# Compressed attention in 49 steps of 128 queries over both images, the local value bias in the output bias, value rows and late casts on ScalarE

## What is computed

```python
blk = mean of feat over 8 x 8 blocks                      # 49 per image
_, idx = lax.top_k(scores, 4); K_sel = blk[idx]
y_cmp = _mha(Q, blk, blk, wq_w[0], ..., pj_w[0], pj_b[0])  # 8 heads of 16 channels, softmax over 49
y_sel = _mha(Q, K_sel, K_sel, wq_w[1], ..., pj_b[1])       # softmax over 4
q = _lin(Q, wq_w[2], wq_b[2]); k = _lin(patches, wk_w[2], wk_b[2]); v = _lin(patches, wv_w[2], wv_b[2])
y_win = _lin(softmax(q k * scale) v, pj_w[2], pj_b[2])     # each pixel to its 7 x 7 neighbours
g = softmax(_lin(_ln(Q), g_w, g_b))
y = g[..., 0:1] * y_cmp + g[..., 1:2] * y_sel + g[..., 2:3] * y_win + Q
```

## Time and profile before

| | us |
|---|---|
| median of three runs (lowest to highest) | 770.14 (766.46 to 771.43) |
| the profiled execution: device time, span of its instructions | 772.19, 770.4 |
| busy in the span: TensorE, VectorE, ScalarE, GpSimd | 689.2, 607.4, 351.2, 214.8 |
| gates and projections end, first maximum of the compressed attention | 121.1 |
| last add of the compressed attention ends | 330.9 |

### The profile page before, as it was taken

The page is one execution under the profiler, slowest core; times in us unless marked ns, Lnnn a source line. Parts: engine busy times, 40 slices in busy tenths (PEclk is TensorE's granted clock), DMA queues, the critical chain, the costliest instruction groups (busy, mean ns, idle before and its releaser), DMA issues.

```text
span 770.4 us, 14139 instructions
## 1 busy us (share of the span) xinstructions
PE 689.2 (89%) x5055; PEld 365.3 (47%) x5055; DVE 607.4 (79%) x1236; ACT 351.2 (46%) x618; POOL 214.8 (28%) x331
## 2 busy tenths in 40 slices
PE   4998987789788989878999999999889999999996
PEld 2543443445344444444555555555434545455553
DVE  6996657878788799867777777777369879999873
ACT  2175423444444344305555555555534062646676
POOL 2026112545445454507100110010190436400000
PEclk9999988979999899969999999999999999999998
DMA  6004221533233339724656656762000000000101
GB/s 245 0 0 109 54 54 45 132 80 79 71 81 93 81 95 252 176 72 131 158 154 180 180 156 167 181 171 47 18 2 0 1 0 0 1 21 22 42 22 63
DMA packets 52663, 66.22 MB, mean 86 GB/s; under 512 B 10606, under 2 KB 48498, under 8 KB 50738
## 3 DMA queue, kind: packets, MB, share of 16 engines
q1 hardware_dynamic: 49426, 43.08, 21.3%
q10 hardware_dynamic: 3168, 22.24, 10.5%
HBM read 43.03 MB, written 21.57 MB: 84 GB/s over the span
## 4 chain that ended last, share of the span: by engine, by line
PE 50%; DVE 22%; issue 8%; ACT 6%; DMA 2%; POOL 1%; SPq 0%; ACTq 0%; DVEq 0%; POOLq 0%
PE banks L959 12%; PE banks L897 7%; PE banks L881 6%; PE banks L840 5%; DVE AC L1204 4%; DVE mx L1392 4%; PE banks L914 3%; DVE sm L1407 2%; DVE X L1484 2%; PE banks L852 2%; DVE SEB L1395 1%; PE banks L710 1%; ACT pf L1022 1%; ACT PTB L1067 1%; PE banks L782 1%
## 5 line engine op out<-in xcount | busy, mean ns | idle before, releaser
L1083 ACT ACTIVATE P<-banks 126x480 f32<-126x480 f32 (+2 forms) x196 | 101.1, 521 | 112.1 <-PE banks L881 98.6
L959 PE MATMUL banks<-FP,PTB 128*128 128x392 f32 x384 | 129.8, 493 | 2.1 <-DVE c L1487 1.2
L1456 DVE TENSOR_REDUCE wn<-banks 128x4 f32<-128x728 f32 x112 | 102.1, 913 | 26.0 <-PE banks L840 24.2
L1204 DVE SCALAR_TENSOR_TENSOR AC<-XT,vec,AC 128x1540 f32<-128x1540 f32 (+5 forms) x48 | 118.0, 2462 | 1.1
L959 PEld LDWEIGHTS banks<-FP,PTB 128*128 128x128 f32 x384 | 72.7, 190 | 56.9 <-DVE FP L1524 2.2
L549 POOL TENSOR_TENSOR SEB<-SEB,rg 112x392 f32<-112x392 f32 x112 | 61.2, 567 | 111.2 <-DVE rg L1414 111.2
L1058 ACT ACTIVATE SEB<-SEB 112x424 f32<-112x424 f32 x56 | 31.2, 558 | 113.1 <-DVE SEB L1395 113.1
L897 PE MATMUL banks<-P,Vw 126*17 126x120 f32 (+2 forms) x1568 | 73.3, 260 | 0.0
L519 POOL TENSOR_TENSOR pk<-pr,pk 128x434 bf16<-128x434 f32 (+1 forms) x42 | 47.7, 1136 | 45.4 <-DVE pk L1307 45.4
L804 PE MATMUL banks<-PTB,VP 106*128 106x448 f32 x112 | 54.0, 570 | 6.2 <-issue 3.7
L782 PE MATMUL banks<-Af,XT 128*112 128x424 f32 x112 | 54.2, 568 | 0.0
(11 more groups left out here) (247 smaller groups left out, 1195.6 us busy)
## 6 DMA issues: line engine op xcount, KB each, us to landing
k_parts<-pk SPq DMA_DIRECT2D x84, 108.5 KB, 3.4
Vw<-v_rows SPq DMA_DIRECT2D x84, 66.9 KB
q_parts<-pk SPq DMA_DIRECT2D x42, 112.0 KB, 2.3
K<-k_parts ACTq DMA_DIRECT2D x7, 651.0 KB, 5.8
v_rows<-vst SPq DMA_DIRECT2D x14, 263.5 KB
X<-in_x SPq DMA_DIRECT2D x2, 1568.0 KB, 8.3
K<-k_parts ACTq DMA_DIRECT2D x7, 434.0 KB, 3.7
out_y<-zs SPq DMA_DIRECT2D x7, 392.0 KB, 2.4
```

The lines of the kernel that those rows point to most:

```text
L959: last = mm(bank(2 + place_in_unit, C, ZPIX), WT[:, dy, part, C * grp:C * (grp + 1)], D[:, part, QROWS * q + dy:QROWS * (q + 1) + dy, :].r ...
L1083: a(P[q % 4][0:BKEYS[b], 0:4 * BQ[b]], PS[0:BKEYS[b], 4 + q % 2, 0:4 * BQ[b]], ACT.Exp).then_inc(sem("w_exp"), 1)
L1204: return ve.scalar_tensor_tensor(out=o, in0=src(ro + dy, rn, co + dx, cn), scalar=v(wcol + t), in1=o, op0=ALU.mult, op1=ALU.add)
L1456: ve.tensor_reduce(dst, src, AX.X, ALU.max, negate=True).then_inc(sem("w_slot_read"), 1)
```

## The change

- The compressed attention runs over both images as one row of 6272 pixels, in 49 tiles of 128 (`QT`), in groups of four tiles (512 columns, one bank); the last group has one tile, and one tile and one group have pixels of both images, and take their matmuls in two parts. `G`, the gates' transposes and logits follow: 13 groups instead of 14 bands.
- The local value bias is no longer added to each value row. As softmax weights sum to one, it is folded through the output projection into that projection's bias row, by two small matmuls and one add before the stage. `BV2` goes.
- Value rows are copied by ScalarE (no bias, one instruction per group), and ScalarE takes the second part's cast of late keys, two steps behind the projection; the third part on GpSimd stands three steps behind, as do the stores.
- Late jobs, keys and values in one list (`LATE_TURN`), stand in 37 steps and take banks 6 and 7 in turn. The residual stands behind the maxima and subtraction in VectorE's step. `pr` has four buffers.

The core of the diff:

```diff
+QT = 128
+CT = IMAGES * PIX // QT
+GROUP = 4
-        LATE_STEPS = 40
-        late_at = {NGJ + n: n * LATE_STEPS // NLATE for n in range(NLATE)}
-        vlate_at = {late_at[NGJ + j * 7 // 4]: j for j in range(NVJ)}
+        LATE_STEPS = 37
+        LATE_BANKS = (6, 7)
+        LATE_TURN = "kkvkkvkkvkv"
+        late = []
+        for n in range(NPJ - NGJ + NVJ):
+            kind = LATE_TURN[n % len(LATE_TURN)]
+            number = sum(which == kind for which, _, _ in late) + (NGJ if kind == "k" else 0)
+            late.append((kind, number, n * LATE_STEPS // (NPJ - NGJ + NVJ)))
...
@@ TensorE
-                    mm(bank(0, 124, C), ones[0:1, 0:124], row[0:1, 2 * C:3 * C], start=True, stop=True)
+                    for u in range(2):
+                        mm(bank(0, VH, C), v(V_FOLD + VH * u, VH), w("pj2", C, C * u), start=(u == 0), stop=(u == 1))
...
+                for n, kind, number in late_jobs(step):
+                    if n < 2:
+                        pe.wait_ge(sem("proj_read"), NGJ)
+                        pe.wait_ge(sem("g_stored"), NCG)
+                    elif late[n - 2][0] == "k":
+                        pe.wait_ge(sem("proj_read"), late[n - 2][1] + 1)
+                    else:
+                        pe.wait_ge(sem("v_ready"), late[n - 2][1] + 1)
+                    if kind == "k":
+                        project(number, LATE_BANKS[n % 2])
+                    else:
+                        values(number, LATE_BANKS[n % 2])
...
@@ ScalarE
+            def late_second(n):
+                cols = pjobs[n][3]
+                act.wait_ge(sem("residual"), n + 1)
+                a(pk[n % RING][:, SLOT[1], 0:cols], pr[n % RING][:, 0:cols], ACT.Copy).then_inc(sem("late_second"), 1)
+            def value_rows(j, b0):
+                vm, g, k = vjobs[j]
+                act.wait_ge(sem("vals"), j + 1)
+                if j >= 2:
+                    act.wait_ge(sem(f"v_stored{j % 2}"), 16 * (j // 2))
+                o = vst[j % 2][:, 0:k, :].rearrange("p t (j d) -> p (t j) d", d=VH)[:, :, 0:DH]
+                a(o, PS[0:124, b0, 0:C * k].rearrange("p (t d) -> p t d", d=DH), ACT.Copy).then_inc(sem("v_ready"), 1)
...
@@ VectorE
-            def value_rows(j):
...
-                for t in range(k):
-                    last = ve.tensor_tensor(o[:, HEADS * t:HEADS * (t + 1), :], i0[:, HEADS * t:HEADS * (t + 1), :],
-                                            BV2[:].rearrange("p (j d) -> p j d", j=HEADS), ALU.add)
-                last.then_inc(sem("v_ready"), 1)
...
-                    link(ve.tensor_copy(BV2[:], PS[0:124, 0, 0:C]))
+                    bias_row = W[0:VH, WCOL["pj2"]:WCOL["pj2"] + C]
+                    link(ve.tensor_tensor(bias_row, bias_row, PS[0:VH, 0, 0:C], ALU.add))
```

More of the change, by code:

```diff
@@ L819, in _, with scores @@
-            run_loop(pe, c_body, BANDS, True)
-            pe.wait_ge(sem("c_added"), NGRP)
+            def scores(s):
+                if s >= 2:
+                    pe.wait_ge(sem("c_sub"), s - 1)
+                for img, lo, hi in image_parts(QT * s, QT * (s + 1)):
+                    o = PS[lo - QT * s:hi - QT * s, s % 2, 0:SC]
+                    mm(o, XTB[:, lo:hi], Af[img][:], start=True, stop=False, skip_group_check=True)
+                    last = mm(o, on3[:, 0:hi - lo], E3[img][:], start=False, stop=True, skip_group_check=True)
+                last.then_inc(sem("c_s"), 1)
@@ new lines, in turned, with folded_values @@
+            def turned(s):
+                pe.wait_ge(sem("c_norm"), 2 * s + 2)
+                if s >= 2:
+                    pe.wait_ge(sem("c_pt"), s - 1)
+                for j in range(PAIRS):
+                    last = tr(bank(2 + s % 2, KC, QT, QT * j), Pn[s % 2][:, KC * j:KC * (j + 1)], ident)
+                last.then_inc(sem("c_tr"), 1)
+            def folded_values(g, j):
+                cols = group_cols(g)
+                if j == 0:
+                    if g == 1:
+                        pe.wait_ge(sem("g_rows"), 1)
+                    pe.wait_ge(sem("c_pt"), min(GROUP * (g + 1), CT))
+                    if g >= 2:
+                        pe.wait_ge(sem("c_added"), g - 1)
+                for part, (img, lo, hi) in enumerate(image_parts(cols.start, cols.stop)):
+                    last = mm(bank(4 + g % 2, C, hi - lo, lo - cols.start), VP[img][:, j, :], PT[g % 2][:, j, lo - cols.start:hi - cols.start],
+                              start=(j == 0 and part == 0), stop=(j == PAIRS - 1), skip_group_check=True)
+                if j == PAIRS - 1:
+                    last.then_inc(sem("c_vp"), 1)
@@ new lines, in _ @@
+            for step in range(C_STEPS):
+                if tile_at(step, 0) is not None:
+                    scores(step)
+                if tile_at(step, TURN_LAG) is not None:
+                    turned(step - TURN_LAG)
+                for g, j in vp_at.get(step, ()):
+                    folded_values(g, j)
+                for n, kind, number in late_jobs(step):
+                    if n < 2:
[7 more added lines that the diff above has]
+                        project(number, LATE_BANKS[n % 2])
+                    else:
+                        values(number, LATE_BANKS[n % 2])
+                if step == 1:
+                    pe.wait_ge(sem("gates"), 1)
+                    tr(bank(TURN_BANK, CT, QT), G[:, :, 2], ident).then_inc(sem("g_turned"), 1)
@@ L823, in _ @@
+            pe.wait_ge(sem("c_added"), NCG)
             pe.wait_ge(sem("masks"), 16 * 2 * BUFS)
```

431 lines of the change are left out of this document (192 added, 239 removed).

## The result

The changed kernel takes 729.75 us (median of 4 runs, 727.30 to 730.72) against 769.21 us (766.46 to 771.43): a ratio of 0.948, 95% interval 0.944 to 0.952. The profiled execution took 729.38 us, with a span of 727.6. The forecast was 728, and its range, 716 to 743, holds the result. But two of its sums are off by about 5 us each, in opposite directions: the stage ends 4.6 us earlier than foretold, and the part behind it is 5.7 us longer.

A forecast was written before the change was run, and what follows sets the result against it. VectorE and a loop of waits bound the steps with late jobs, VectorE the rest. 120.3 + 128 + 27.7 + 10 = 286 us for the stage's end, 45 less; 772.2 - 45 gives 727, plus 1 traffic: 728 us, range 716 to 743.

The forecast's parts named there:

- TensorE paces the first part: Steps with late key and value jobs mixed in: TensorE longest, 128 us for 37 steps; likeliest case, 0.69.
- Its sum, 119.3: TensorE's work in the 37 steps with late jobs, if it never waits: 119.3 us, 3.22 a step.
- The allowance of 9 us: Added to TensorE's 119.3 us: 3 for the low clock at the start, 6 for steps where VectorE is late.
- VectorE's sum, 102: VectorE's work in the 37 steps: 137.55 less 26.6 for casts and additions, less four steps of 2.35: 102 us.
- ScalarE's sum, 91: ScalarE's work in the 37 steps, with late casts and value copies added: 91 us, so TensorE stays longest.
- the 14.2 us of waiting for the high part: VectorE's wait for ScalarE before residuals, expected to vanish once residuals stand behind the next step's maximum and subtraction.
- the step's length from latencies: Rival: 4.02 us a step comes from loop latencies, so 37 steps cost 149; 749 us, cases between 738 and 752; 0.15.
- Start, second part and end: First maximum at 120.3; 11 steps after the late jobs, 27.7 us; last maximum to last add into XT, 10 us.
- The store ring: Four high-part buffers, reused after stores: slack 2 to 3 us, cost 0 to 5 us, within the likeliest range.
- What is late next: Window start: mask loads land at + 36.1 after tile 37's maximum, first window matmul at + 38.9; fits by 2.8 us.
- The window "as it is": Window stage and the rest: left unchanged, 1 us (0 to 4) added for load traffic; wrong if changed over 4 us.
- Slower by the low clock: Rival: shorter waits keep TensorE at its lower clock while late jobs run, 119.3 becoming 239; some 839 us; 0.02.

The follow-up runs named there:

- the two cuts: Changed kernel without the small second matmul of each tile's scores: 715.3 us; changed kernel with late residuals covering 16 of 434 columns: 727.3 us.
- the second set of runs: The changed kernel run once more, unedited, for a second profile: median 722.97 us.
- all undone: Changed kernel, still 49 tiles, with value rows and casts back on VectorE, residual first and one bank per kind: 751.0 us.
- seven steps fewer: Changed kernel with its late jobs spread over 30 steps in place of 37, still four buffers: 744.0 us.
- one bank for each kind: Changed kernel with late jobs in one bank for keys and one for values, instead of two in turn: 734.8 us.
- less VectorE work: Changed kernel with each late residual computing 16 of its 434 columns: 727.3 us.

## Why the prediction was right, point by point

**TensorE paces the first part: right, shown** by the two cuts and its busy share of 97%. Its sum, 119.3, measured 121.07 busy.

**The allowance of 9 us on that sum was too large.** 124.41 - 121.07 = 3.3 us are idle. The 6 us for steps in which VectorE is late are the term that was mis-sized: TensorE waited 1.7 us for GpSimd and 1.6 for ScalarE, and never for VectorE. The 3 us for the start are nearer: 7.94 us at a clock of 0.76 lose some 1.9 (an estimate from these two figures), about what lies between 119.3 and 121.07. That steps with a residual and an add into XT are followed by lighter ones, and that two scores' lead absorbs the difference, is argued, not shown.

**VectorE's sum, 102, was too low:** 108.6. Of this 3.4 us are the residuals, 777 ns each in place of 650, for which the last section has the cause. The rest is in the subtraction: it took 26.6 us away, the durations of casts and additions added up, but an instruction starts before the one ahead of it has ended, as in the kernel before:

```profile
165.99 0.88 DVE L1318 TENSOR_TENSOR vst<-banks,BV 124x128 f32<-124x128 f32 x4
166.78 0.38 DVE L1307 CAST pk<-pr 128x434 bf16<-128x434 f32 x1
167.07 0.61 DVE L1302 TENSOR_TENSOR pr<-pf,pk 128x434 f32<-128x434 f32 x1
```

Four additions of 0.28 us take 0.79 of the list, the cast 0.29. With both kinds of work back VectorE is busy 18.8 us longer, while its residuals are 3.0 shorter (672 ns each): the two cost it some 22 us (an estimate from these figures), and not 26.6. ScalarE's sum, 91, was too high mostly for the same reason: it was busy 85.85, and without the 28 casts 12.2 less, where their durations add up to 15.

**ScalarE's prices** were near: late cast 549 ns for 580, value copy 583 for 600. Where the Trainium skill's rule ("ScalarE: Activation LUTs", Rules for kernel authors: adds and the like belong on VectorE) was weighed, the sum by it was 129 us on VectorE and 129 to 137 for the first part. With both kinds of work back it was 140.9, so here the move pays, against the rule. But the reason given, VectorE's length, is only part of it: VectorE was busy 127.3 of these, and alone the casts cost 2.8 us, the value rows 8.7. What ScalarE gives, it seems, is a reader that is not at the end of a long step; a reader earlier in VectorE's step was not run. For the casts alone, 2.8 us of the first part are too little for the medians to tell.

**Where the gain came from was told too simply.** The prediction let the 14.2 us of waiting for the high part "vanish" and gave the step's length from latencies 0.15. The residual's place alone is worth 21 us and the two banks in turn 9.7, about as much as the work moved (16.4). The rival's mechanism is real: with the residual first the step is 3.94 us with no engine full, nearly the 4.02 of before. It did not come true because the change takes that loop apart, as the prediction argued of each edge. The parts do not add up (21 + 9.7 + 16.4 = 47, all undone 28.3): each edge that is put back brings long waits back by itself (31.1 us of VectorE for the high part, 8.6 of TensorE for its reader in one bank).

**Start, second part and end.** First maximum 119.06 for 120.3; second part 27.77 for 27.7; last maximum to last add 10.18 for 10. The last add ends at 281.4 for 286: 4.6 us early, of which 3.6 are the first part.

**The store ring: no cost here, and close.** ScalarE never waited for a store in the first part. The slack of 2 to 3 us was rightly called small: seven steps fewer turn it into 20.9 us of waiting.

**What is late next: right.** The last of the masks was issued at 262.3 and landed 18.2 later, 280.5, 2.2 us ahead of the first window matmul (2.8 foretold):

```profile
L457 SPq DMA_DIRECT2D Q<-in_cmask x2: 452/490/527, 257.4 to 262.3; - x2
...
DMA to landing us min/median/max: 5.2/11.1/18.2
```

**The window "as it is": the term that failed.** The prediction added 1 us (0 to 4); the part behind grew by 6.7 in this profile, and by 2.4 in the other. By the prediction's own test this part was not to change by more than 4 us, and in the first profile it did. The growth makes up for the stage's 4.6, so that 728 comes so near is luck: the second set of runs has 723.0, inside the range and 5 below its centre. What grew, one late transfer in some executions, is in the last section.

**Slower by the low clock: not so.** The clock in the first part rose from 0.91 to 0.98. Before the change it did not fall behind each long wait, but behind three of TensorE's four waits for value rows: right behind them it was 0.50, 0.63 and 0.65 (waits of 3.31, 2.78 and 3.30 us), and 1.00 after the one of 2.38.

**Two slips without weight.** In the forty slices before the change the two engines stand at seven to nine tenths, not at eight or nine. And by the prediction's own chances (0.69, 0.10 and half of 0.15 inside) the range leaves out some 14 in 100, not 2 in 10.

## What to carry to other kernels

Relieving the busiest engine pays little unless the order then lets the next engine run ahead (with the work moved and the residual in its old place the first part was 145.6 us, against 152.8 with nothing moved): look for instructions that stand ahead of the work another engine waits for, and for a buffer whose reader sits at the end of a long step. Where two engines take turns, no engine is full in the table of busy times, so the sum over the longest engine is a lower bound and the loop has to be followed in the timeline. Before concentrating jobs in fewer steps, work out the buffer ring's slack: here a ring too small cost 22.9 us, half of the stage's gain. And when you take work off an engine in a sum, count the time from its start to the next instruction's, since durations overlap.

## What the runs showed of the hardware

**A subtraction on VectorE waits for GpSimd.** In the changed kernel residuals take 0.60 us when GpSimd is idle and up to 1.34 us when its third part has just begun:

```profile
163.03 1.01 POOL L543 TENSOR_TENSOR pk<-pr,pk 128x434 bf16<-128x434 f32 x1
163.17 1.34 DVE L1354 TENSOR_TENSOR pr<-pf,pk 128x434 f32<-128x434 f32 x1
```

GpSimd ends at 164.04, the residual 0.47 us later, so it does its work only then. The Trainium skill ("SBUF — State Buffer", Who interferes with whom) says that a VectorE instruction with two SBUF inputs contends with a GpSimd one that reads SBUF, and that whichever comes second is blocked; the trace agrees. Before the change one of 28 residuals took over 0.7 us; in the changed kernel 11 did, each begun while a third part ran, which accounts for the 127 ns by which the mean grew. The new place behind the subtraction is not what does it: in the run with the residual first 15 of 28 are that long. The changed kernel and all its edits have the third part a step later in GpSimd's list than the kernel before; no run tests that alone. As VectorE had time to spare, it cost nothing that shows.

**One late small transfer costs 4 to 5 us in some executions.** The part behind the window's start was 436.7 to 440.6 us in eleven profiles and 444.5 to 445.4 in three (changed kernel, one bank for each kind, less VectorE work). In each of the three, 4 to 5 us are lost at the same job, the fourth of fourteen: from the third job's output matmuls to the fifth's it is 35.1 to 35.4 us, and 30.4 to 31.1 in the eleven. TensorE waits there for a small transfer into `Q` from `nT` (2.90, 2.69 and 2.05 us), its granted clock falls (0.57 from 375.46 to 379.40 us in the changed kernel), and the four output matmuls behind (line 949) take 3.0 to 3.4 us; in the second profile of the changed kernel they take 1.77.

```profile
375.46 0.58 PE L916 MATMUL banks<-Q,K 128*128 128x120 bf16 x4 [2.90 <-DMA Q<-nT]
...
376.32 3.02 PE L949 MATMUL banks<-ON,W 128*128 128x448 f32 x4
```

```profile
370.65 1.77 PE L949 MATMUL banks<-ON,W 128*128 128x448 f32 x4
```

What makes that transfer late in one execution and not in the next stays open: it does not follow the place of the loads, since of the changed kernel one profile has it and the other has not. Nor does the length of the wait decide alone: in the second profile TensorE waits 2.12 us for such a transfer at 316.12, another job, and the clock stays at 1.00 behind it. Between these two profiles of one and the same kernel, 729.4 and 723.6 us, 4.3 of the 5.8 us lie behind the stage, nearly all at this job, and 1.65 ahead of it, where the first maximum comes at 119.06 and 117.41.
